# Scores and row maxima as four 64x64 matmuls in place of two 64x128 ones

## What is computed

```
xn   = group_norm(x)                       # 256 channels, 64*64 = 4096 positions
qkv  = qkv_weight @ xn + qkv_bias
q, k, v: 4 heads of 64 channels, each (64, 4096)
attn = einsum('bhdk,bhdq->bhkq', q, k) / 8 # 4096 x 4096 for each head
attn = softmax(attn, axis=-1)
out  = einsum('bhkq,bhdq->bhdk', attn, v)
x    = x + proj_weight @ out + proj_bias
```

## Time and profile before

| | before |
|---|---|
| median of 3 runs | 2934.8 us |
| profiled execution | 2934.27 us |
| its span, first to last instruction | 2932.5 us |
| TensorE (PE) busy | 2793.7 us, 95% |
| VectorE (DVE) busy | 2117.5 us, 72% |
| GpSimd (POOL) busy | 2027.3 us, 69% |
| ScalarE (ACT) busy | 1402.7 us, 48% |
| mean granted TensorE clock | 0.988 of full speed |

### The profile page before, as it was taken

One profiled execution on the slowest core, in us unless ns is written; L12 is line 12 of the kernel. 1 busy time (PEld: TensorE's weight loads), 2 busy tenths in 40 slices (PEclk: granted clock), 3 DMA queues, 4 the chain that ended last, 5 costly groups with the idle time before them and its releaser, 6 DMA issues. The chain is left out here.

```text
span 2932.5 us, 43630 instructions
## 1 busy us (share of the span) xinstructions
PE 2793.7 (95%) x17060; PEld 1013.2 (35%) x17060; DVE 2117.5 (72%) x2496; ACT 1402.7 (48%) x1477; POOL 2027.3 (69%) x1208
## 2 busy tenths in 40 slices
PE   5899999998999999998999999989999999799898
PEld 3333333333333333343333333343333333244343
DVE  5688888726777888456788888267777885588785
ACT  3355555553555555533555555534555555254342
POOL 2588888893888888844888888947888888500022
PEclk9999999999999999999999999999999999999999
DMA  5000000001000000041000000010000000421022
GB/s 213 35 1 1 1 1 1 1 5 60 1 1 1 1 1 1 1 153 42 1 1 1 1 1 1 1 44 1 1 1 1 1 1 1 148 79 60 15 100 86
DMA packets 26820, 78.27 MB, mean 27 GB/s; under 512 B 1921, under 2 KB 2177, under 8 KB 25601
## 3 DMA queue, kind: packets, MB, share of 16 engines
q1 hardware_dynamic: 25792, 74.19, 7.3%
q10 hardware_dynamic: 832, 1.45, 0.1%
HBM read 58.86 MB, written 16.78 MB: 26 GB/s over the span
## 5 line engine op out<-in xcount | busy, mean ns | idle before, releaser
L512 POOL TENSOR_TENSOR acc_pool<-acc_pool,prob 128x512 f32<-128x512 f32 (+1 forms) x992 | 1781.0, 1795 | 297.5 <-ACT prob L567 177.0
L803 DVE TENSOR_REDUCE m_part<-ps 128x2 f32<-128x1024 f32 x1024 | 1250.6, 1222 | 479.8 <-PE ps L662 456.0
L567 ACT ACTIVATE prob<-ps,exp_scale 128x1024 f32<-128x1024 f32 x1024 | 1086.9, 1111 | 1015.7 <-PE ps L719 1007.8
L703 PE MATMUL ps<-prob,vals 128*64 128x512 f32 x4096 | 990.9, 605 | 0.0
L662 PE MATMUL ps<-k_hi,q_hi 64*128 64x512 f16 x2048 | 394.3, 383 | 45.3 <-DVE m_part L803 45.3
L703 PEld LDWEIGHTS ps<-prob,vals 128*64 128x64 f32 x4096 | 248.7, 136 | 501.9 <-issue 364.2
L714 PE MATMUL ps<-q_hi,k_hi 64*128 64x512 f16 x2048 | 391.1, 379 | 0.0
L714 PE MATMUL ps<-q_hi,k_lo 64*128 64x512 f16 x2048 | 390.4, 378 | 0.0
L719 PE MATMUL ps<-m_rows,shift 64*128 64x512 f16 x2048 | 389.9, 377 | 0.4
L714 PE MATMUL ps<-q_lo,k_hi 64*128 64x512 f16 x2048 | 390.2, 378 | 0.0
L869 DVE TENSOR_TENSOR ps<-ps,prob 128x512 f32<-128x512 f32 x480 | 331.5, 691 | 72.4 <-ACT prob L567 72.4
(11 more groups left out here) (109 smaller groups left out, 1408.3 us busy)
## 6 DMA issues: line engine op xcount, KB each, us to landing
xt<-in_x SPq DMA_DIRECT2D x40, 512.0 KB, 4.3
xf<-in_x SPq DMA_DIRECT2D x4, 2048.0 KB, 16.5
x_scratch<-y_tile SPq DMA_DIRECT2D x16, 512.0 KB, 5.0
wf<-in_w_t SPq DMA_DIRECT2D x4, 1152.0 KB, 8.9
rows<-x_scratch SPq DMA_DIRECT2D x8, 576.0 KB, 5.3
rows<-x_scratch SPq DMA_DIRECT2D x8, 544.0 KB, 4.6
xn<-in_x SPq DMA_DIRECT2D x8, 512.0 KB, 5.6
xt<-x_scratch SPq DMA_DIRECT2D x4, 1024.0 KB, 5.1
```

Of the source, the lines that this page charges most:

```text
L512: nc.gpsimd.tensor_tensor(acc[:, part], acc[:, part], tile[:, part], ALU.add).then_inc(pool_add, 1)
L567: nc.scalar.activation(prob[:, n % PBUF], g.ps_s[:, kt % 2].rearrange("p h n -> p (h n)"), ACT.Exp, scale=g.exp_scale[:]).then_inc(exp_don ...
L703: last = mm(g.ps_o[own[h], :], vals[:, kt, own[h]], prob[:, n % PBUF, h * TB:(h + 1) * TB], start=(kt == 0), stop=(kt == KT - 1))
L803: v.tensor_reduce(m_part[:, block % 2, :, u], where[i] if where else g.ps_max, AX.X, ALU.max).then_inc(mx_used, 1)
```

## The change

Each of the score matmuls and of the maximum matmuls, which had 64 rows and 128 columns, is cut into two with 64 rows and 64 columns. The first writes PSUM partitions 0 to 63, the second 64 to 127. The streamed operand (512 columns) is the same for both. With the two heads there are thus four matmuls, one for each quarter of the array, where there were two. Nothing else is changed: order, waits and all other engines' programs are the same, and `then_inc` stays on the last matmul of a set.

```diff
@@ maximum
                 for h in range(2):
-                    last = mm(into[:, h], q_hi[own[h], block * TB + t * P:block * TB + (t + 1) * P],
-                              k_hi[own[h], kb * TB:(kb + 1) * TB], start=True, stop=True)
+                    for side in own:
+                        first = block * TB + t * P
+                        last = mm(into[side, h], q_hi[own[h], first + side.start:first + side.stop],
+                                  k_hi[own[h], kb * TB:(kb + 1) * TB], start=True, stop=True)
                 last.then_inc(mx_ready, 1)
@@ scores
-                keys = slice(kt * P, (kt + 1) * P)
                 for k, q in ((k_hi, q_hi), (k_lo, q_hi), (k_hi, q_lo)):
                     for h in range(2):
-                        mm(g.ps_s[:, kt % 2, h], k[own[h], keys], q[own[h], cols(qb)], start=(k is k_hi and q is q_hi),
-                           stop=False)
+                        for side in own:
+                            keys = slice(kt * P + side.start, kt * P + side.stop)
+                            mm(g.ps_s[side, kt % 2, h], k[own[h], keys], q[own[h], cols(qb)],
+                               start=(k is k_hi and q is q_hi), stop=False)
                 if kt == 0:
                     pe.wait_ge(m_rows_done, (it + 1) * 2)
                 for h in range(2):
-                    last = mm(g.ps_s[:, kt % 2, h], shift[own[h]], m_rows[own[h], qb % 2], start=False, stop=True)
+                    for side in own:
+                        last = mm(g.ps_s[side, kt % 2, h], shift[own[h], side], m_rows[own[h], qb % 2],
+                                  start=False, stop=True)
                 last.then_inc(s_ready, 1)
```

## The result

The changed kernel takes 2946.84 us (median of five runs, 2944.51 to 2947.55), the kernel before 2934.89 (five runs, 2934.6 to 2935.26): a ratio of 1.0038, 95% interval 1.0027 to 1.0049 (the quotient of the two medians, 1.0041, lies inside it). It is 12 us slower, where 15 were forecast. Beside the filled kernels of the second set of experiments it was run once more, 2946.2 against 2935.53, ratio 1.0035 [1.0021, 1.0048].

A forecast was written before the change was run, and what follows sets the result against it. PE was taken to bound the query stage. 508 switch pairs x (0.015 load + 0.01 skew) = 12.7 us, plus 2 us in projections, made +15 us on 2934.3: 2949, forecast 2950 us, range 2932 to 2995.

The forecast's parts named there:

- Does the switch go away?: Between float16 sets and values: rows still differ, so both drains stay whole, 0 us saved.
- The set itself: Score and maximum sets: four matmuls and loads instead of two, step unchanged at 0.215 us.
- Rivals 2, 3 and 4: In each set: loads late, 3080 to 3210 us, 7%; quarters not four at once, 4035 us, 4%; instruction supply, 3%.
- rival 4: In each set: eight instructions can't be supplied fast enough, set takes 0.43 us, 4035 us; chance 3%.
- The bare load: First float16 load behind a switch, uncovered: 0.026 us for 64 columns, +0.015 us against the kernel before.
- The skew: Staggered starts of a set's four matmuls, drain before values waits for the last: +0.01 us per switch pair.
- The projection stages: 128 more pairs of switches at the maximum units there, 3.2 us if PE bound, taken as 2 us.
- The sum: Whole kernel: 12.7 us from 508 switch pairs plus 2 us from projections, together +15 us.
- The price of the switches: In each group of two key tiles, drains and bare loads both ways sum to 0.257 us.
- Rival 1: At the 508 switch pairs: switch is free when columns agree, -130 us, 2805 us; chance 6%.

The follow-up runs named there:

- filled kernels: Kernel before and changed kernel, each with idle matmuls in TensorE's pauses at the query stage starts: 2927.38 us (ratio 0.9971) and 2940.02 us (ratio 1.0017).
- all-64x64 run: Changed kernel with values product and column sums reading only partitions 0 to 63, so scores, maxima and values are all 64x64: 2846.33 us, ratio 0.9696.
- scores-only run: Kernel before with only the scores cut into 64x64, maxima staying 64x128: 3031.92 us, ratio 1.0327.

## Why the prediction was right, point by point

- **Does the switch go away? No.** The forecast rested on the earlier trace rows: rows alone, columns alone and both cost 0.09 to 0.10 us. Way in and way out after are 0.32 and 0.52 us, as predicted. The doubt that was left, that the earlier trace rows mixes a change of rows with one of number format, is settled by the all-64x64 run: format costs nothing. That columns alone cost a switch stands in the scores-only run too, within float16.
- **The set itself.** Unchanged at 0.216 us, with four matmuls side by side. Rivals 2, 3 and 4 all fall on this one row. For rival 4 it says more than L700 could: eight instructions in 0.216 us, 27 ns each, kept up over eight sets.
- **The bare load.** Taken as 0.026 us from half of the float32 row, measured 0.024. Halving float32's price was right to 2 ns, but it is no rule: for 128 columns it would give 52 ns, where 11 were measured. The Trainium skill's figure for 64 columns (TensorE: Matmul & The Clock Gate, section LDWEIGHTS, 53 ns) is twice the 24 ns that a bare load adds here, and half of the 107 ns that its row in the trace lasts; the measurement decides. That column tiling turns fast weight load off, as the Trainium skill says (TensorEngine Tiling (Array Packing), section Restrictions), agrees with the loads: 107 ns for 64 columns against 95 for 128.
- **The skew.** Taken as +0.01 us; it is about 0.007 (the last of four starts 10 ns behind the first, where the last of two started 3 to 4). Load and skew gave 0.018 in the groups against the 0.025 forecast, 9.1 us instead of 12.7. The part that I had too high is this skew and some 2 ns that each way out got shorter.
- **The projection stages.** Taken as 2 us, measured 2.4 in the three stretches between the query stages of the filled pair.
- **The sum.** 9.1 and 2.4 make 11.5, where 12.7 and 2 were forecast. That the first pair of profiles also comes near (13 us) is in part luck: the half clock adds there what the stretches between the stages lack.
- **The price of the switches.** 0.257 us by the four rows; before's group minus the group without any switch is 4.132 - 3.875 = 0.257.
- **Rival 1's gain**, put at 130 us for the day that the switch were free, was 90 in the all-64x64 run, as the other engines stand. A bound that is taken away moves the end only as far as the next one; I had named VectorE as that next one without pricing it, and GpSimd not at all.

A version with all modes equal that computes everything was not tried. Built as the scores are, where each half of the rows writes a PSUM bank of its own, it would take one more bank for the lower 64 keys' values product, and scores (four), maxima (two), outputs and the shared tile take all eight. Whether it could do with one bank was not tried either.

## What to carry to other kernels

Before making one property of two kinds of matmul agree, look in the trace for a pair that differs in that property alone and a pair that doesn't differ at all: here they priced the idea at zero before anything was built. A mode of the array is rows and columns together, and in every pair seen here a change of either costs 0.09 to 0.10 us and a bare load. Where TensorE pauses, look at the granted clock behind the pause; matmuls without use in the pauses of 1.4, 0.9 and 3.6 us were worth 8 us here.

## What the runs showed of the hardware that was not expected

- A bare float16 load of 64 columns takes 24 ns, one of 128 columns in 64x128 mode 11 ns: the smaller one is the slower. The scores-only kernel has both side by side (400 and 387 ns against 376). Float32 takes 51 ns for 64 columns and 105 for 128.
- With all modes equal, the two halves of the rows ran 0.18 us apart for whole groups without any loss: they did not wait for each other.
- After the same pause, the half clock (the 1.2 GHz level) lasted 6.8, 10.2 or 13.7 us in different query stages of one changed kernel, and 6.8 in each of the four of the profiled kernel before. It doesn't go with the change: the kernel before with half the rows in values has 10.2 us at two of its starts, and the changed kernel run again 6.8 at two. What decides it was not settled; the filled kernels don't have it at the four starts.
